# A transformer tower in fp32 on one core: a new opening and a new order of TensorE's work in stage A

## What is computed

```python
h = patches @ W + b                                    # 64 x 45 x 128
x1 = layernorm(h);  xp = pad(layernorm(x1) * gamma + beta)
q, k, v = split(xp @ w_qkv)                            # 8 heads of 16
a = softmax(q @ k.T)                                   # attn1 = attn2 = attn3 here
z = a.T / (max(sum(abs(a), -1)) * max(sum(abs(a), -2)))   # maxima over everything
for _ in range(6):
    xz = a @ z
    z = 0.25 * z @ (13*I - xz @ (15*I - xz @ (7*I - xz)))
out = a @ (z @ (a @ v)) + conv33(v)
h = h + x1 + out @ w_out + b_out
h = h + mixture_of_experts(layernorm(h))               # 8 experts, top 2
```

## Time and profile before

| what | us |
|---|---|
| median of 3 runs | 607.26 (606.39 to 610.11) |
| profiled execution | 611.33, of which the span of the trace 609.52 |
| PE busy | 568.2 (93%) |
| DVE busy | 423.0 (69%) |
| ACT busy | 317.0 (52%) |
| POOL busy | 312.0 (51%) |
| stage A with its opening, by the trace | 0 to 159.56 |
| bridge | 159.56 to 170.23 |
| stage B | 170.23 to 609.5 |

### The profile page before, as it was taken

How to read it: one execution, slowest core, us unless ns; L and a number is a source line. 1 busy time by engine, 2 the same in 40 slices (tenths; PEclk the granted TensorE clock), 3 DMA queues, 4 the chain that set the end, 5 groups by cost and what they waited for, 6 DMA issues and landing times. The chain is left out here.

```text
span 609.5 us, 39484 instructions
## 1 busy us (share of the span) xinstructions
PE 568.2 (93%) x16991; PEld 430.8 (71%) x16991; DVE 423.0 (69%) x1097; ACT 317.0 (52%) x663; POOL 312.0 (51%) x451
## 2 busy tenths in 40 slices
PE   1799999999889889999999999999999999989996
PEld 1577777788556668787787777777777877756663
DVE  4446666665146537869879789789799799577764
ACT  1356666666567735747647657656557567010000
POOL 2767766666146735746646656655655665000000
PEclk9969999999799989999999999999999999999998
DMA  2410000100000001122213223122222122114431
GB/s 62 135 31 11 12 12 12 29 2 2 2 4 1 11 23 42 35 71 61 68 50 79 60 52 75 51 60 67 60 59 71 48 63 67 51 50 109 106 79 36
DMA packets 35607, 29.27 MB, mean 48 GB/s; under 512 B 4108, under 2 KB 35044, under 8 KB 35556
## 3 DMA queue, kind: packets, MB, share of 16 engines
q1 hardware_dynamic: 30660, 24.52, 15.6%
q0 software_dynamic: 672, 2.12, 1.2%
q10 hardware_dynamic: 4224, 2.01, 1.2%
HBM read 27.07 MB, written 1.57 MB: 47 GB/s over the span
## 5 line engine op out<-in xcount | busy, mean ns | idle before, releaser
L479 POOL TENSOR_TENSOR T<-Q,W 128x368 f32<-128x368 f32 x192 | 182.6, 970 | 143.3 <-issue 125.3
L629 ACT ACTIVATE Q<-P 64x368 f32<-64x368 f32 x384 | 195.4, 509 | 111.5 <-DVE P L840 98.7
L985 PEld LDWEIGHTS bank<-P 46*46 46x46 f32 x6144 | 148.6, 120 | 37.8 <-issue 33.5
L985 PE MATMUL bank<-P 46*46 46x46 f32 x6144 | 162.3, 207 | 6.6 <-issue 3.3
L985 PE MATMUL bank<-W 46*46 46x46 f32 x6144 | 161.0, 207 | 2.6 <-issue 2.6
L985 PEld LDWEIGHTS bank<-W 46*46 46x46 f32 x6144 | 146.4, 120 | 3.0 <-issue 2.9
L840 DVE SCALAR_TENSOR_TENSOR P<-T,bank 128x368 f32<-128x368 f32 x160 | 85.1, 532 | 37.7 <-PE bank L985 37.4
L830 DVE SCALAR_TENSOR_TENSOR W<-Q,bank 128x368 f32<-128x368 f32 x192 | 101.9, 531 | 13.1 <-PE bank L985 12.0
L985 PE MATMUL bank<-xnT,w1c 128*128 x168 | 63.3, 500 | 0.0
L985 PE MATMUL bank<-hT,w2c 128*128 128x360 f32 x168 | 61.9, 491 | 0.3
L927 DVE SCALAR_TENSOR_TENSOR hT<-bank,b_sb,E 128x360 f32<-128x360 f32 x86 | 46.8, 586 | 9.5 <-PE bank L985 8.0
(11 more groups left out here) (140 smaller groups left out, 784.0 us busy)
## 6 DMA issues: line engine op xcount, KB each, us to landing
E<-wrow SPq DMA_DIRECT2D x43, 180.0 KB, 3.1
w2c<-in_L_ffn_w SPq DMA_DIRECT2D x42, 128.0 KB, 2.1
w1c<-in_L_ffn_w SPq DMA_DIRECT2D x42, 128.0 KB, 2.0
X<-wrow SPq DMA_DIRECT2D x21, 180.0 KB, 3.3
w_sb<-in_L_ffn_w POOLq DMA_DIRECT2D x2, 1024.0 KB, 7.6
pat<-in_x SPq DMA_DIRECT2D x24, 60.0 KB
out<-outb ACTq DMA_DIRECT2D x24, 60.0 KB
wqkv_sb<-in_L_attn_w_qkv ACTq DMA_DIRECT2D x1, 192.0 KB, 2.7
```

What stands on the lines that cost most here:

```text
L479: pool.tensor_tensor(out=T[g], in0=Q[g], in1=W[g], op=ALU.add).then_inc(s_t[g], 1)
L629: ins = act.activation(Q[g][to, :, :], P[g][fro, :, :], ACT.Copy, scale=T_IN)
L985: return pe.matmul(out, lhsT, rhs, start=start, stop=stop, skip_group_check=True)
```

## The change

- *Loads.* ACT issues tok_w and tok_b with a semaphore of their own (`s_tw`), then w_qkv, a small activation, then b_out and w_out. SP issues gamma and beta behind the first three patch loads. `s_wa` counts four loads.
- *Opening of PE.* It waits for three cleared banks only (DVE clears bank 3, 0, 2 first), runs four products of 128 columns (WARM_P), patches and embed of block 0, then waits for the eight banks and the four loads and runs five `keep_warm` (WARM_Q) before normed. ACT waits for the four loads behind the first patches; DVE waits for `s_tw` alone; POOL makes the first roots before its wait.
- *PE's order of a group.* Scores stand ahead of the turn. `keep_warm` stands between turn and products, at g = 1 alone; in the last block at each group. It was behind the products at g = 0, 1, 3.
- *k rows.* DVE copies kT (`keys`), at g = 3 between normalise and subtract; ACT's copy is gone.
- *POOL.* x1 at g = 1, h0 plus bias at g = 2, the sum at g = 3.
- *Bridge.* In place of the all-reduce PE transposes the two columns of `den` into one row (two products), DVE takes the maximum, multiplies and inverts on one partition, PE spreads RHO times that over the partitions by a product. Six paddings, split 1, 2, 3. The bias products go to bank 7, and their wait moves.

```diff
-WARM_A, WARM_B, WARM_C = 1, 5, 1
+WARM_A, WARM_C, WARM_P, WARM_Q = 1, 1, 4, 5
+WARM_B = (1, 2, 3)
...
             load_patches(0)
+            sp.dma_start(gam_sb[:, :], gamma.unsqueeze(1)).then_inc(s_wa, 16)
+            sp.dma_start(bet_sb[:, :], beta.unsqueeze(1)).then_inc(s_wa, 16)
             sp.dma_start(kraw[:, :], res_k.rearrange("h a k b -> h (a k b)")).then_inc(s_kraw, 16)
...
             pool.wait_ge(s_init, N_INIT)
+            roots(0)
             pool.wait_ge(s_wa, 16 * N_WA)
-            roots(0)
             residual(0)
+            with_bias(0)
+            residual_sum(0)
...
                     if g == 0 and more:
                         roots(blk + 1)
+                    if g == 1 and more:
+                        residual(blk + 1)
                     if g == 2 and more:
-                        residual(blk + 1)
+                        with_bias(blk + 1)
+                    if g == 3 and more:
+                        residual_sum(blk + 1)
...
-            pool.wait_ge(s_den, 2)
-            pool.partition_all_reduce(den2[:, :], den[:, :], 128, RMAX).then_inc(s_den2, 1)
...
             act.dma_start(wqkv_sb[:, :], w_qkv).then_inc(s_wa, 16)
+            act.wait_ge(s_init, 1)
+            act.activation(lamc[:, :], normT[:, 0, 0:1], ACT.Copy)
             act.dma_start(bout_sb[:, :], b_out.partition_broadcast(128)).then_inc(s_wa, 16)
...
-                act.wait_ge(s_k, blk + 1)
-                act.activation(kT[:, :, :], bank[3][:, 0:BW].rearrange("p (b n) -> p b n", b=BB),
-                               ACT.Copy).then_inc(s_qk, 1)
...
-            act.wait_ge(s_wa, 16 * N_WA)
             act.wait_ge(s_init, N_FIRST)
             patches(0)
+            act.wait_ge(s_wa, 16 * N_WA)
             normed(0)
...
-            for bk in bank:
+            for bk in [bank[n] for n in (3, 0, 2, 1, 4, 5, 6, 7)]:
                 dve.memset(bk[:, :], 0.0).then_inc(s_psum, 1)
...
-            dve.wait_ge(s_wa, 16 * N_WA)
+            dve.wait_ge(s_tw, 16 * N_TW)
+            dve.memset(rho_row[:, :], RHO).then_inc(s_m2, 1)
...
+            def keys(blk):
+                dve.wait_ge(s_k, blk + 1)
+                dve.tensor_copy(kT[:, :, :], bank[3][:, 0:BW].rearrange("p (b n) -> p b n", b=BB)).then_inc(s_kT, 1)
...
                     normalise(i, g % 2)
+                    if more and g == 3:
+                        keys(blk + 1)
                     if more or g < 3:
                         subtract(i + 1, (g + 1) % 2)
...
-            dve.tensor_tensor(out=dprod[:, :], in0=den2[:, 0:1], in1=den2[:, 1:2], op=ALU.mult).then_inc(s_dmax, 1)
+            dve.reduce_max(m2[:, :], bank[4][0:1, 0:256].rearrange("p (c n) -> p c n", c=2), AX.X).then_inc(s_dmax, 1)
             dve.wait_ge(s_dmax, 2)
+            dve.tensor_tensor(out=dprod[:, :], in0=m2[:, 0:1], in1=m2[:, 1:2], op=ALU.mult).then_inc(s_dmax, 1)
...
-            pe.wait_ge(s_psum, 8)
+            pe.wait_ge(s_psum, 3)
...
                 if g == 0:
-                    pe.wait_ge(s_qk, 3 * blk + 3)
+                    wait_apart(pe, met, (s_qk, 2 * blk + 2), (s_kT, blk + 1))
...
+            for _ in range(WARM_P):
+                mm(bank[3][:, 0:128], ident, ident)
+            patches(0)
+            pe.wait_ge(s_tw, 16 * N_TW)
+            embed(0)
+            pe.wait_ge(s_psum, 8)
             pe.wait_ge(s_wa, 16 * N_WA)
-            patches(0)
-            embed(0)
+            for _ in range(WARM_Q):
+                keep_warm()
             normed(0)
...
-                    if late:
-                        turn(i - 1, (g - 1) % 2)
                     if g < 3:
                         scores(blk, g + 1)
                     elif more:
                         scores(blk + 1, 0)
+                    if late:
+                        turn(i - 1, (g - 1) % 2)
                     if more and g == 0:
                         embed(blk + 1)
-                    if more and g == 2:
+                    elif more and g == 2:
                         normed(blk + 1)
+                    elif g == 1 or not more:
+                        keep_warm()
                     if late:
                         products(i - 1, (g - 1) % 2)
...
-                    if g != 2:
-                        keep_warm()
...
-            for _ in range(WARM_B):
-                mm(bank[5][:, :], ident, w1_sb[:, 0:2, :].rearrange("p e f -> p (e f)"))
+            bridge(WARM_B[0])
+            pe.wait_ge(s_den, 2)
+            mm(bank[4][0:1, 0:128], den[:, 0:1], ident)
+            mm(bank[4][0:1, 128:256], den[:, 1:2], ident).then_inc(s_den2, 1)
+            bridge(WARM_B[1])
+            pe.wait_ge(s_m2, 2)
+            mm(bank[4][:, 256:257], rho_row[:, :], drec[:, :]).then_inc(s_den2, 1)
+            bridge(WARM_B[2])
             pe.wait_ge(s_bz, EXPERTS)
...
-                    wait_apart(pe, met, (s_acc, blk), (s_gv, 2 * blk + 2), (s_b2r, 1))
+                    wait_apart(pe, met, (s_acc, blk), (s_gv, 2 * blk + 2))
...
+            pe.wait_ge(s_b2r, 1)
             with pe.Fori(1, BLOCKS) as blk:
```

More of the change, by code:

```diff
@@ L39 @@
 AX = mybir.AxisListType
-RMAX = bass.bass_isa.ReduceOp.max
 B, L, C = 64, 375, 8
@@ L196, in tower @@
         den = sb("den", [128, 2])
-        den2 = sb("den2", [128, 2])
-        dprod = sb("dprod", [128, 1])
-        drec = sb("drec", [128, 1])
+        m2 = sb("m2", [1, 2])
+        rho_row = sb("rho_row", [1, 128])
+        dprod = sb("dprod", [1, 1])
+        drec = sb("drec", [1, 1])
         lamc = sb("lamc", [128, 1])
@@ L235, in tower @@
         outb = sb("outb", [TT, TILES, D])
+        s_tw, s_m2, s_kT = sem("s_tw"), sem("s_m2"), sem("s_kT")
         s_cn, s_wa, s_wb, s_wc = sem("s_cn"), sem("s_wa"), sem("s_wb"), sem("s_wc")
@@ L270, in tower @@
                                                sem("s_d4"), sem("s_out"))
-        N_WA, N_WC = 6, 6
+        N_TW, N_WA, N_WC = 2, 4, 6
         N_FIRST, N_INIT = 4, 11
@@ L397, in residual, with with_bias @@
                 ins.then_inc(s_x1, 1)
+            def with_bias(blk):
                 pool.tensor_tensor(out=h0b[:, :, :], in0=h0[:, :, :],
@@ L400, in residual, with residual_sum @@
                                    op=ALU.add).then_inc(s_hb, 1)
+            def residual_sum(blk):
                 pool.wait_ge(s_hb, blk + 1)
@@ L506, in _ @@
             act.dma_start(cn[:, :], consts).then_inc(s_cn, 16)
[L507 to L510, removed]
+            act.dma_start(tokw_sb[:, :], tok_w).then_inc(s_tw, 16)
+            act.dma_start(tokb_sb[:, :], tok_b.partition_broadcast(128)).then_inc(s_tw, 16)
             act.dma_start(wqkv_sb[:, :], w_qkv).then_inc(s_wa, 16)
+            act.wait_ge(s_init, 1)
+            act.activation(lamc[:, :], normT[:, 0, 0:1], ACT.Copy)
             act.dma_start(bout_sb[:, :], b_out.partition_broadcast(128)).then_inc(s_wa, 16)
@@ L526, in normed, with queries @@
                                ACT.Identity, bias=bet_sb[:, 0:1], scale=gam_sb[:, 0:1]).then_inc(s_normT, 1)
-            def queries_keys(blk):
+            def queries(blk):
                 q = bank[2][:, 0:BW].rearrange("p (b n) -> p b n", b=BB)
@@ L566, in _ @@
             act.wait_ge(s_cn, 16)
-            act.wait_ge(s_wa, 16 * N_WA)
             act.wait_ge(s_init, N_FIRST)
             patches(0)
+            act.wait_ge(s_wa, 16 * N_WA)
             normed(0)
-            queries_keys(0)
+            queries(0)
             values(0)
@@ L581, in body @@
                     if more and g == 3:
-                        queries_keys(blk + 1)
+                        queries(blk + 1)
                     if not (first and g < 2):
@@ L793, in _ @@
             norms(0)
+            keys(0)
             subtract(0, 0)
@@ L807, in _ @@
             dve.wait_ge(s_den2, 1)
-            dve.tensor_tensor(out=dprod[:, :], in0=den2[:, 0:1], in1=den2[:, 1:2], op=ALU.mult).then_inc(s_dmax, 1)
+            dve.reduce_max(m2[:, :], bank[4][0:1, 0:256].rearrange("p (c n) -> p c n", c=2), AX.X).then_inc(s_dmax, 1)
             dve.wait_ge(s_dmax, 2)
-            dve.reciprocal(drec[:, :], dprod[:, :]).then_inc(s_dmax, 1)
+            dve.tensor_tensor(out=dprod[:, :], in0=m2[:, 0:1], in1=m2[:, 1:2], op=ALU.mult).then_inc(s_dmax, 1)
             dve.wait_ge(s_dmax, 3)
-            dve.tensor_scalar(lamc[:, :], drec[:, :], RHO, None, ALU.mult).then_inc(s_lamc, 1)
+            dve.reciprocal(drec[:, :], dprod[:, :]).then_inc(s_m2, 1)
+            dve.wait_ge(s_den2, 2)
+            dve.tensor_copy(lamc[:, :], bank[4][:, 256:257]).then_inc(s_lamc, 1)
             dve.memset(top[:, :, :], 0.0).then_inc(s_mix, IDLE + 2)
             dve.wait_ge(s_b2p, 1)
-            dve.tensor_tensor(out=b2_sb[:, :], in0=bank[4][0:EXPERTS, 0:D], in1=b2_sb[:, :], op=ALU.add).then_inc(s_b2r, 1)
+            dve.tensor_tensor(out=b2_sb[:, :], in0=bank[7][0:EXPERTS, 0:D], in1=b2_sb[:, :], op=ALU.add).then_inc(s_b2r, 1)
             dve.wait_ge(s_band, 16 * 2)
@@ L1109, in _, with bridge @@
```

(12 more changed lines are left out.)

## The result

The changed kernel is slower: 616.59 us in the median (614.57 to 621.10, 4 runs) against 608.61, a ratio of 1.0144 with a 95% interval of 1.0076 to 1.0213. Its profiled execution took 615.86 us with a span of 614.06. The forecast was 596 and a range up to 604. Of the likeliest case the opening came as forecast; the mechanism of rival (a), that the clock falls in the loop, is what happened, and it cost more than the change had won.

A forecast was written before the change was run, and what follows sets the result against it. The prediction took the loop as bound by PE's work, partly padding, and both ends by chains of waits. Savings of 4.8 + 1.5 + 3.3 + 1.6 + 0.3 = 11.5 us took 607.3 to 596 us, range 592 to 604.

The forecast's parts named there:

- likeliest case: Whole kernel: the granted clock stays at 1.00 in the loop; median 596 us, own range 592 to 599, chance 0.55.
- the opening: Start up to the first scores: earlier patches and table load, with pads in idle time, less 4.8 us (bounds 3.0 to 5.5).
- rival (a): Loop: the clock falls once or twice, each costing 3 to 4 us; 600 to 604 us, chance 0.25.
- first scores: End of the opening: PE starts the first block's scores at 18.1 us instead of 22.9.
- first block: From its first scores to the next block's: less 1.5 us, bounds nothing and less 5 if the clock stays.
- a block at full clock: Loop of six whole blocks: 15.9 us each instead of 16.45, together less 3.3 us.
- last block at full clock: Last block's first scores to stage A's last product: 17.7 us against 19.29, less 1.6 (0.5 to 2.5).
- bridge: Between stage A's last product and stage B: all-reduce gone, six paddings instead of five, less 0.3 us (plus 1 to less 2).
- (c): Loop: the clock falls at the boundary of every block, at 4 us each; slower, 624 us, chance 0.07.
- the wait for k: Block boundary: scores straight after v wait for DVE's k copy, ending 0.25 us after v's (estimate 0 to 0.5).
- two of three `keep_warm` go in every full block: less 1.5: Loop: two paddings of 0.75 us each removed from PE per full block, saving 1.5 us a block.
- The price of a fall: Loop: some 0.4 us lost per microsecond at half clock, so 3 to 4 us for each fall of the clock.

The follow-up runs named there:

- first variant: The changed kernel with one `keep_warm` more per full block, at g = 3 between turn and products: 600.48 us, ratio 0.9899 to the kernel before the change.
- bridge variant: The first variant without the bridge's last three pads and with VectorE's bands written ahead of its wait for the bias products: 597.91 us, ratio 0.9886.

## Why the prediction was wrong

Point by point, forecast against the trace of the change:

| step | forecast | measured |
|---|---|---|
| first scores | 18.1 | 18.46 |
| first turn | 23.9 | 23.71 |
| first block | less 1.5 | less 3.5 (15.18 us) |
| a block at full clock | 15.9 | 16.04 to 16.14 |
| loop's half clock | none | 3.4 and 17.1 us: plus 8.6 |
| last block at full clock | 17.7 | 18.28 (first variant) |
| last block's half clock | none | 13.7 us: plus 5.9 |
| bridge | less 0.3 | plus 0.7 |
| stage B | nothing | plus 0.6 |

*The step that failed* is the choice of the likeliest case, "the clock stays", with 0.55, against 0.25 for rival (a) and 0.07 for (c). I had named the place (scores, turn, a hole of 0.75 us at the last group) and it is where the clock fell: the measured hole is 0.80 us. What I set against it, that the hole is smaller than the 0.86 us of the earlier trace rows and that the wait for k might be nil, did not carry. The wait for k played no part: it was 0.37 us ahead of the scores of 33.64, behind which the clock stayed, and nil ahead of the three falls. Nor did the hole lead to a fall each time, but at three boundaries of seven.

The term that was wrong by this is "two of three `keep_warm` go in every full block: less 1.5". I had counted the pads as work alone. As work the sum was nearly right (16.0 to 16.1 us a block at full clock against 15.9), but with g = 3 left open the clock fell, and filling it again brought the loop's clock from 0.90 to 1.00 and the time from 616.6 to 600.5. (The rule of the Trainium skill, "TensorE: Matmul & The Clock Gate", section "HAM oscillation — how this bites in real kernels", that only an idle gap several times as long makes the clock fall, is not what these runs show: no hole ahead of the three falls was longer than 0.80 us, and filling it stopped them.)

*The price of a fall* was mis-sized too, by its length. 0.4 us lost per microsecond was right (0.41); I had taken 7 to 10 us of half clock as in the kernel before, so 3 to 4 us. The change paid 1.5, 7.1 and 5.9. What ends such a stretch is not shown: from 88.9 to 101.3 PE was busy without a gap and stayed at half clock, and the clock came back at 105.9 during the products for v, at 58.1 and 157.1 during `products`. So rival (a), "600 to 604", was too cheap as well: three falls made 14.5 us. Counted from the profiled execution, the forecast was 599.8; with 14.5 and the 1.5 us by which the other rows of the table differ from the forecast that gives 615.8, and 615.86 was measured. Counted from the median forecast of 595.8 the same terms give 611.8; of the 4.8 us up to the measured 616.6, 1.4 are the higher median of the kernel before (608.61 where it was 607.26), and the rest stays unexplained.

*The first block* was put 2 us too long: I took its half clock as before (some 10 us), and it had 3.4 us.

*The bridge* was mis-sized: I counted six pads at full clock against five at a mean of 0.86 and let the two small products and the spreading one cost nothing. They stand on PE between the pads (0.60 and 0.38 us). That the all-reduce itself was not on the path was right: it went, and the bridge did not get shorter.

*Right* were the opening with each of its marks (within 0.4 us), the table load's 1.28 us with the activation 0.01 us behind it (4.50), GpSimd's six issues as what made X of group 0 late, the holes at each group (0.80, 0.49), and the gain of VectorE's k copy in sign. The pads of the opening carry much of its gain: without them 0.9 of 7.9 us was left in the trace, which is that of the longest of its ten executions. Two slips of the prediction change nothing in its sum: the terms of the last block add up to 17.6 and not 17.7, and the remark that a drain would have made the opening gain 1.4 us more does not follow, since the copy's old start, 9.96, is a measured one.

*Open:* stage B had 0 to 17 us at half clock near its second block in these kernels (17.1 in the change, 6.8 before, none in the bridge variant's trace). PE stalls there for 1.1 to 1.9 us in each of these traces, also in the bridge variant's (1.23), where the clock stayed; what decides on it was not tried. It was not tried either why the first block has 3.4 us at half clock in one execution and 13.7 in another with the same program there, why four of the seven boundaries stayed without a fall, or whether a second pad elsewhere in the block, with the hole left open, would hold the clock.

## What to carry to other kernels

A pad of matmuls that lies in a wait is free, and taking it out can cost far more than its length (here one of 0.84 us in each full block: 12 us in all). Before removing padding, list PE's idle holes in the new order; a hole as long as one behind which the trace already shows a fall of the clock is a risk, and a price taken from the trace before can be too low (its longest stretch at half clock in stage A was 10.2 us, the change's 17.1). Put the pad into the hole itself, between the turn and the products; under the new order no run here tried it behind them. In the opening, pads ahead of PE's first real work can pay too: here by some 4 us by the ratios (their intervals overlap) and 6.9 in the execution that was traced.

## What was not expected of the hardware

- Fewer instructions, more time: without its last pad TensorE did less work in the loop, and the kernel took 628.5 instead of 616.6 us.
- In the change PE was busy without a gap for 12.4 us (88.9 to 101.3) and stayed at 1.2 GHz all the while.
- Moving one pad of 0.84 us from one group to another moved the time by 12 us, with the work unchanged.
- At half clock the durations of scores, turn and products grew by factors of 1.70, 1.79 and 1.65, those of ScalarE's and VectorE's steps not at all (XT 0.58, row maximum 0.52 to 0.54 us on both sides).
